# Reordering the groups of products in the slots of a fused attention and feed-forward kernel

## The reference

```
xn = layernorm(x)
qkv = xn @ w_qkv.T                  # 32 query heads, 4 key and value heads, 64 wide
q, k = rope(q), rope(k)             # each key and value head serves 8 query heads
scores = q k^T / 8, causal          # 256 x 256 for each head
attn = softmax(scores)
out = (attn @ v) @ w_o.T            # back to (4, 256, 256)
x = x + out + ffn(xn)               # layer 1; layer 0 has the same outline
```

## Time and profile before

| | us |
|---|---|
| median of 3 runs | 379.31 |
| lowest and highest run | 378.7, 380.05 |
| the profiled execution, time | 380.41 |
| the profiled execution, span of the core | 378.5 |
| PE busy in the span | 361.6 |
| weight loads (PEld) busy | 337.0 |
| DVE busy | 301.3 |
| POOL busy | 294.5 |
| ACT busy | 251.2 |

### The profile page before, as it was taken

How to read it: one execution, slowest core, us unless ns; L and a number is a source line. 1 busy time by engine, 2 the same in 40 slices (tenths; PEclk the granted TensorE clock), 3 DMA queues, 4 the chain that set the end, 5 groups by cost and what they waited for, 6 DMA issues and landing times.

```text
span 378.5 us, 8337 instructions
## 1 busy us (share of the span) xinstructions
PE 361.6 (96%) x2808; PEld 337.0 (89%) x2824; DVE 301.3 (80%) x685; ACT 251.2 (66%) x806; POOL 294.5 (78%) x260
## 2 busy tenths in 40 slices
PE   8998879998999999999999999999999999999996
PEld 3677768997889999999999999999999999998985
DVE  5867988866887788879777888887788879788883
ACT  1378755565788666767767676767666777767671
POOL 5536867789999999999999899999996988775000
PEclk9999989999999999999999999999999999999999
DMA  7997000632334446334443663344455533334200
GB/s 255 416 406 314 28 30 0 162 92 56 99 97 112 125 104 165 84 85 111 112 114 86 169 165 100 100 106 102 127 117 165 134 90 84 86 86 106 62 0 29
DMA packets 35516, 46.20 MB, mean 122 GB/s; under 512 B 4625, under 2 KB 27410, under 8 KB 35090
## 3 DMA queue, kind: packets, MB, share of 16 engines
q1 hardware_dynamic: 35328, 45.66, 41.8%
q10 hardware_dynamic: 146, 0.00, 0.0%
HBM read 13.14 MB, written 1.05 MB: 37 GB/s over the span
## 4 chain that ended last, share of the span: by engine, by line
PE 81%; DVE 10%; ACT 5%; DMA 2%; issue 1%; SPq 0%; DVEq 0%
PE bank L1345 18%; PE bank L1055 13%; PE bank L1253 12%; PE bank L1366 12%; PE bank L1305 10%; PE bank L1212 3%; PE bank L1311 3%; PE bank L1188 3%; PE bank L1308 2%; PE bank L1064 2%; DMA wq0T<-in_L_attn_w_qkv_dram 2%; ACT bank L534 2%; PE bank L1269 2%; DVE stats L782 1%; ACT probT_hi L543 1%
## 5 line engine op out<-in xcount | busy, mean ns | idle before, releaser
L534 ACT ACTIVATE bank<-bank,neg_max 128x256 f32<-128x256 f32 (+1 forms) x256 | 101.1, 396 | 8.1 <-DVE neg_max L968 7.9
L543 ACT ACTIVATE probT_hi<-bank 128x512 fp32r<-128x512 f32 x96 | 57.7, 601 | 65.7 <-PE bank L1055 65.6
L968 DVE TENSOR_REDUCE neg_max<-bank 128x2 f32<-128x512 f32 (+1 forms) x96 | 66.0, 688 | 26.8 <-PE bank L1311 15.7
L1345 PE MATMUL bank<-probT_hi,v 128*128 128x256 f32 x384 | 76.5, 295 | 1.4 <-DVE oT_lo L996 0.7
L984 DVE TENSOR_TENSOR prob<-bank,rsum 128x512 f32<-128x512 f32 x96 | 66.4, 691 | 3.3
L990 DVE TENSOR_TENSOR probT_lo<-bank,probT_hi 128x512 fp32r<-128x512 f32 x96 | 65.4, 681 | 0.6 <-ACT probT_hi L543 0.4
L1305 PE MATMUL bank<-kT,qT 128*128 128x256 f32 (+1 forms) x384 | 62.6, 272 | 0.0
L1345 PEld LDWEIGHTS bank<-probT_hi,v 128*128 128x128 f32 x384 | 58.7, 189 | 4.2 <-issue 2.3
L1055 PE MATMUL bank<-cst,prob 128*128 128x128 f32 x384 | 57.9, 273 | 3.6 <-DVE prob L984 2.6
L699 POOL TENSOR_TENSOR rope_b<-turned,cst 128x512 f32<-128x512 f32 x36 | 46.5, 1292 | 13.0 <-DMA turned<-raw 11.9
L1305 PEld LDWEIGHTS bank<-kT,qT 128*128 128x128 f32 x384 | 55.0, 191 | 0.0
(11 more groups left out here) (165 smaller groups left out, 792.5 us busy)
## 6 DMA issues: line engine op xcount, KB each, us to landing
turned<-raw SPq DMA_DIRECT2D x72, 128.0 KB, 2.0
qT<-q_hi SPq DMA_DIRECT2D x64, 128.0 KB, 2.4
qT<-split_lo SPq DMA_DIRECT2D x64, 128.0 KB, 2.4
wq0T<-in_L_attn_w_qkv_dram SPq DMA_DIRECT2D x4, 512.0 KB, 8.0
wout<-in_L_attn_w_out_dram SPq DMA_DIRECT2D x4, 512.0 KB, 13.0
nat_qkv<-in_L_attn_w_qkv_dram SPq DMA_DIRECT2D x2, 1024.0 KB, 20.9
nat_o<-in_L_attn_w_o_dram SPq DMA_DIRECT2D x1, 2048.0 KB, 21.5
kT<-split_hi SPq DMA_DIRECT2D x16, 128.0 KB, 2.4
```

The source lines that it names most:

```text
L534: ins = nc.scalar.activation(own, own, ACT.Exp, bias=neg_max[it % 2][:, first + j:first + j + 1], accum_out=sums[it % 2][:, first + j:firs ...
L543: nc.scalar.activation(probT[0][:, n % 4, :], bank[2 + n % 2][:, :], ACT.Copy).then_inc(t_hi, 1)
L968: dve.tensor_reduce(neg_max[n // UNITS % 2][:, unit_columns(n % UNITS)], score_bank(n)[:, :].rearrange("p (h k) -> p h k", h=heads), AX.X, ...
L1345: ins = pe.matmul(group_bank(), v[b % 2][:, DH * z:DH * z + P], p, start=m == 0, stop=m == last)
```

## The change

In a slot, PE now issues F and O before H. ACT and DVE empty bank 4 of a group one slot later in their program: at the head of the slot that follows H's (on DVE behind that slot's `maxima`, ahead of `normalise`), instead of near the end of H's own slot. For H of slot 96 and 98, behind the last scores, they keep the old place; the group of slot 95 is emptied at the head of slot 96. The hunks stand in the order ACT, DVE, PE.

```diff
+        def group_ahead(n):
+
+            return group_at(n - 1) if 1 <= n <= N_UNITS else None
+
+        def group_behind(n):
+
+            return group_at(n) if n >= N_UNITS else None
...
             def slot(n):
+                if group_ahead(n):
+                    heads_hi(*group_ahead(n))
                 if 2 <= n < N_UNITS + 2:
                     probs_T(n - 2)
                 if n < N_UNITS:
                     probs(n)
-                if group_at(n):
-                    heads_hi(*group_at(n))
+                if group_behind(n):
+                    heads_hi(*group_behind(n))
                 if n < N_UNITS:
                     empty(fills_at(n // UNITS, n % UNITS))
...
                 if n < N_UNITS:
                     maxima(n)
+                if group_ahead(n):
+                    heads_lo(*group_ahead(n))
                 if 1 <= n < N_UNITS + 1:
                     normalise(n - 1)
                 if 2 <= n < N_UNITS + 2:
                     probs_lo(n - 2)
-                if group_at(n):
-                    heads_lo(*group_at(n))
+                if group_behind(n):
+                    heads_lo(*group_behind(n))
...
                 if 2 <= n < N_UNITS + 2:
                     prob_T(n - 2)
-                if group_at(n):
-                    heads_out(*group_at(n))
                 if n < N_UNITS:
                     fill(fills_at(it, u))
                 if it == ITS and u == 1:
                     project_out(it - 1, 0, (0,))
                 elif it and u in (1, 5):
                     project_out(it - 1, u // 5)
+                if group_at(n):
+                    heads_out(*group_at(n))
```

## The result

| | before | changed |
|---|---|---|
| median, us | 379.04 (378.7 to 380.05, 4 runs) | 382.28 (382.23 to 382.34, 4 runs) |
| profiled execution: time, span | 380.41, 378.5 | 382.28, 380.5 |
| slot 0's first scores to the last products' start (the pipeline) | 281.95 | 284.08 |

What follows compares the result with a forecast made beforehand. PE was taken to bound the kernel. Terms -1.9 - 0.1 - 0.15 + 2.4 + 1.9 = +2.15 us, about 2.1 on a median of 379.31, gave 381.4 us; own range 380.4 to 382.6, 8-in-10 range 379.6 to 383.0.

Steps and rivals of the forecast that it cites:

- order of the pieces, a swapped pair: PE, H swapped with F or O: the extra 0.08 us behind T only moves; pair within 0.02 us of before.
- pauses in slot 5, nine: Slot 5 of nine iterations: O between T and H removes PE's wait for bank 4, 0.21 to 0.22 us each, -1.9.
- iteration 0: Pipeline start: H of g2 gains up to 0.6 us, H of g1 loses 0.4 behind ACT's weight copy; net -0.15.
- bank 6 in slot 4, six: Slot 4 of six iterations: F waits for ACT's copy of slot 3's fill, 0.40 us each, +2.4.
- slot 0 of iteration 15: Pipeline end: no F there, so H of g2 waits for `oT_lo` behind the maxima of unit 90, +1.0 us.
- slot 96: Pipeline end: H of g2 stands directly behind g1 and one T and waits 0.83 us for bank 4.
- The first step: Whole kernel: PE bounds it, 39.86 of 40 us busy; its pauses show only from start to start, 0.59 against 0.35 us.
- rival 4: PE order: groups behind products save 0.08 us, those behind T pay nothing; some 36 places, 2.9 us, 378.5; chance 0.04.
- the first rival: Six slots 4: bank 6 is free in time, F waits for nothing; -2.4 us against the forecast, 379.0; chance 0.12.
- The second rival: Full iterations: DVE's chain ends late and T waits, 0.3 us in 14 iterations, 4 us more, 385.5; chance 0.07.
- rival 3: End costs only 1.2 us and bank 6 only 0.1 a time; -0.3 in all, 379.0; chance 0.07.
- the last one: Whole run: the median, 379.31 us, changes by the same amount as the profiled execution, giving 381.4 us.

Runs made afterwards that it cites:

- experiment 2: The changed kernel with H put back ahead of F in slot 4 only; ratio 1.0019 to the kernel before, pipeline 282.82 us.
- experiment 4: The changed kernel's PE order, but ACT and DVE empty bank 4 within H's slot as before; ratio 1.0032 to the kernel before, pipeline 283.38 us.
- experiment 6: Changed kernel, but emptying within H's slot, H first in slot 4, O in halves in the last two iterations; 377.34 us, ratio 0.9948 to before.
- experiment 3: The changed kernel with the old order and old emptying from slot 4 of iteration 14 on; ratio 1.0023 to the kernel before, pipeline 282.64 us.
- experiment 7: The changed kernel with ACT copying bank 6 ahead of slot 3's exponentials where slot 4 fills k or v; ratio 0.9982 to the kernel before.
- experiment 5: The kernel before with only the emptying of bank 4 moved to the head of the next slot; 409.38 us, ratio 1.0799.
- experiment 8: As experiment 6, but in iterations 14 and 15 O's first half stays whole, its second split between slots 3 and 5; 377.63 us, ratio 0.9948 to before.
- experiment 1: The kernel before run again with no edit; ratio 1.0003, ten runs from 378.76 to 381.71 us.

## Why the prediction was right

Point by point, measured in the changed kernel's slots against the same slots before:

| term | predicted, us | measured, us |
|---|---|---|
| order of the pieces, a swapped pair | within 0.02 | 0.72 + 1.51 against 0.80 + 1.43 |
| pauses in slot 5, nine | -1.9 | -0.20 to -0.22 each, -1.87 |
| shorter pauses | -0.1 | -0.08 |
| iteration 0 | -0.15 | +0.51 - 0.63 = -0.12 |
| bank 6 in slot 4, six | +2.4 | +0.37 each, +2.24 |
| slot 0 of iteration 15 | +1.0 | +1.01, less 0.05 in slot 1 |
| slot 96 | +0.83 | 1.18 - 0.36 = +0.82 |
| T of slot 4, iterations 14 and 15 | +0.08 | +0.09 |
| sum | +2.15 | +2.04 by terms, +2.13 for the pipeline |

The first step, that PE is bound and that its pauses are to be read from start to start, is what the rest hangs on. The nine pauses of 0.24 us appear in no list of the products' waits (the weight loads' list has them, without a cause), and they were there to be gained: experiments 2, 4 and 6 gain all nine, and experiment 3 the seven ahead of its edit. The order itself costs nothing, as said: the extra 0.08 us behind T stays and only changes its piece, which was rival 4's question.

The wait at bank 6 was taken as 0.40 and is 0.35 from T to F, with 0.02 more for a piece behind a wait. The two corrections that I let cancel did not quite: ACT's copy comes 0.09 to 0.10 us earlier, and only 0.05 passes from its end to F. Experiments 2 and 7 show both causes, that F needs the bank and that the copy is queued behind exponentials; the first rival (free in time) fell by 0.35 us. The second rival, DVE late in full iterations, did not come: T waits for `prob` in no slot that it did not before.

The end of the pipeline is the sum of the waits predicted (+1.87 against 1.9, so not rival 3's 1.2). The chain there was right in its parts, and experiment 3 takes them away. What I did not see is how general it is. I reckoned H of g2 in slot 0 of iteration 15 from the maxima, but in what I expected of experiment 5 I counted the same wait only where slot 4 holds no fill, as if any work between two groups covered it. Experiment 5 refutes that. For the changed kernel it made no difference, since O and F stand in H's own slot there, except in one place: iteration 0.

The loss in slot 5 of iteration 0 was forecast from the wrong queue, and its size, 0.4 to 0.5 against +0.51, is luck. The prediction has ACT's copy of weights push back the copy of g0. It does: ACT's copy ends at 104.43. But this slot has nothing between T and H either, and DVE's maxima hold `oT_lo` back almost as long:

```profile
103.79 0.69 DVE L978 TENSOR_REDUCE neg_max<-bank 128x2 f32<-128x512 f32 x1 [0.34 <-PE bank L1323]
104.47 0.42 DVE L1006 TENSOR_TENSOR oT_lo<-bank,oT_hi 128x256 fp32r<-128x256 f32 x1
```

Maxima hold DVE for 0.61 us elsewhere, so without the weight copy `oT_lo` would have started at about 104.40, and T would take the 1.37 us of slot 0 of iteration 15 instead of 1.44 (before 0.93). By this estimate the maxima alone account for all but 0.07 of the 0.51 us.

The forecast time, 381.4, is 0.9 us below the measured 382.28. The terms don't account for it: the spans differ by 2.0 us, as predicted (380.6 against 380.5), and the profiled executions by 1.9. The step that missed is the last one, that the change is the same for the median. The median of before (379.31, later 379.04) stood 1.1 to 1.4 us below its own profiled execution, between the two kinds, while the changed kernel's four executions were all of the longer kind. Had they mixed as before, the median would have come out lower, between some 381.0 and 382.3 us by the 1.3 us between the kinds (an estimate); which kind they held was chance.

Still open: why an execution is of the one kind or the other, and how often the transfers on the instruction queue meet q's DMAs in versions 6, 7 and 8; seven executions of version 8, all of the shorter kind, lie between 376.41 and 377.64 us.

## What to carry to other kernels

When one engine is bound, read its work from start to start and give every piece a length; a pause that is shorter than the pipeline's overlap stands in no list of the products' waits, though the weight loads' list may have it. Of each wait ask two things: what work lies between the release's cause and the waiter in the waiter's queue, and what stands ahead of the releasing instruction in its own. Emptying a bank behind an operation that waits for the bound engine's next work ties the bank to that work, however early the data was ready; here that alone cost 30 us.

## What the runs showed of the hardware that I had not expected

The 1.3 us between the two kinds of execution arise in one spot. Three windows of the kernel before and of the profiled run of experiment 3 (columns as in the earlier trace rows; the clock is the third number from the end, ahead of the DMA share and GB/s):

```profile
48.00:50.00 2.00, 0.35 (x3) 0.15 (x2) 1.86 (x9) 1.58 (x5) 1.95 (x4) 1.00 0.00 0
50.00:52.00 2.00, 1.72 (x9) 1.57 (x10) 2.00 (x6) 0.60 (x1) 0.93 (x1) 0.66 0.35 131
52.00:54.00 2.00, 2.00 (x6) 1.52 (x6) 1.79 (x9) 0.60 (x1) 0.90 (x2) 0.50 0.04 12
```

```profile
48.00:50.00 2.00, 0.08 (x1) 0.02 (x1) 1.89 (x8) 1.32 (x4) 1.96 (x4) 1.00 0.02 7
50.00:52.00 2.00, 1.99 (x12) 1.69 (x13) 2.00 (x5) 1.20 (x2) 0.67 (x1) 1.00 0.36 132
52.00:54.00 2.00, 2.00 (x15) 1.78 (x14) 1.79 (x10) 0.86 (x2) 1.17 (x2) 1.00 0.01 4
```

In both, PE is nearly idle from 48 to 50 us. In one execution the granted clock then falls to 0.50, 1.2 GHz, and 6 products are done from 52 to 54 us; in the other it stays at 2.4 GHz, and 15 are done. Of the ten profiled executions five show the fall in the clock (before, changed, 1, 2 and 6) and five do not (3, 4, 5, 7 and 8). In the first five the pipeline starts between 90.85 and 91.16 us, in the others between 89.57 and 89.73: 1.3 us apart on average, as the times of whole runs are. A few executions lie outside this split, such as one of 380.53 us at a clock of 1.00 and one of 381.63 us at 0.996, and no trace shows why. Two kernels that differ by less than 0.4% can be put in the wrong order by this if each is profiled once and only spans are compared; the stretch behind it compares to 0.03 us, except where a DMA is met as in experiment 8. The Trainium skill, in TensorE: Matmul & The Clock Gate, says that an idle stretch of TensorE throttles its clock and that where this falls is not fixed to the kernel's start, so that the same kernel can differ from run to run; the two traces agree that the same idle stretch is followed by a fall in one execution and not in another, and the price here is 1.3 us.
